# First ffn of a four-layer network: quantized numbers read as 16-bit halves of their words, and the gate products issued ahead of the up products

## The reference

```python
def act_qdq(x):
    qmax = 2.0 ** (ACT_BITS - 1) - 1.0
    scale = jnp.maximum(jnp.max(jnp.abs(x)) / qmax, 1e-12)
    return jnp.clip(jnp.round(x / scale), -qmax - 1.0, qmax) * scale
x = act_qdq(x)
up = act_qdq(x @ lpbq_dequant(w_up).T)
gate = act_qdq(x @ lpbq_dequant(w_gate).T)
sig = fixed_qdq_u16(jax.nn.sigmoid(gate))
gate = act_qdq(gate * sig)
o = act_qdq(gate * up)
return o @ lpbq_dequant(w_down).T
```

## Time and profile before

| | us |
|---|---|
| median of three runs | 1404.43 |
| lowest, highest | 1403.75, 1405.94 |
| the profiled execution | 1409.03 |
| its span on the core | 1407.2 |
| PE busy | 1245.4 (88%) |
| DVE busy | 861.9 (61%) |
| ACT busy | 675.2 (48%) |
| POOL busy | 291.5 (21%) |

### The profile page before, as it was taken

One profiled execution on the slowest core, in us unless ns is written; L12 is line 12 of the kernel. 1 busy time (PEld: TensorE's weight loads), 2 busy tenths in 40 slices (PEclk: granted clock), 3 DMA queues, 4 the chain that ended last, 5 costly groups with the idle time before them and its releaser, 6 DMA issues.

```text
span 1407.2 us, 26467 instructions
## 1 busy us (share of the span) xinstructions
PE 1245.4 (88%) x9327; PEld 964.6 (69%) x9327; DVE 861.9 (61%) x1828; ACT 675.2 (48%) x1358; POOL 291.5 (21%) x502
## 2 busy tenths in 40 slices
PE   3889980688999889999888999899999998898999
PEld 2555630256888889887777888498888754555877
DVE  3879768754456566656676565566554566764242
ACT  1556858545443334444444444234444375665553
POOL 1799400120002233230000013044320111100000
PEclk9999995899999999999999999999999999999999
DMA  8000010131050313104006001032120000000000
GB/s 312 1 2 2 2 75 0 65 137 61 1 202 23 113 46 100 48 25 177 30 1 264 40 7 48 21 111 68 33 94 2 1 2 2 1 2 1 0 15 16
DMA packets 42606, 75.71 MB, mean 54 GB/s; under 512 B 3816, under 2 KB 33520, under 8 KB 41584
## 3 DMA queue, kind: packets, MB, share of 16 engines
q1 hardware_dynamic: 38384, 65.62, 12.7%
q0 software_dynamic: 4096, 8.40, 1.9%
HBM read 59.72 MB, written 14.29 MB: 53 GB/s over the span
## 4 chain that ended last, share of the span: by engine, by line
PE 69%; DVE 15%; ACT 7%; issue 4%; POOL 2%; DVEq 1%; DMA 1%; SPq 0%; ACTq 0%; POOLq 0%
PE bank L1674 7%; PE bank L1663 7%; PE bank L1659 6%; PE bank L1718 5%; PE bank L1650 3%; PE bank L1445 3%; PE bank L1511 3%; PE bank L1728 3%; PE bank L1450 3%; PE bank L1451 2%; PE bank L1452 2%; PE bank L1643 2%; PE bank L1645 2%; PE bank L1644 2%; PE bank L1527 2%
## 5 line engine op out<-in xcount | busy, mean ns | idle before, releaser
L1911 ACT ACTIVATE SC<-bank 128x512 f32<-128x512 f32 x192 | 114.3, 595 | 218.1 <-PE bank L1659 123.3
L1998 DVE SCALAR_TENSOR_TENSOR SC<-bank,SM,SC 128x512 f32<-128x512 f32 x128 | 95.8, 749 | 125.0 <-PE bank L1663 108.6
L1674 PE MATMUL bank<-A,SC 128*128 x1024 | 137.0, 277 | 7.2 <-DVE SC L1998 6.2
L1663 PE MATMUL bank<-X,SC 128*128 128x128 f32 x1024 | 136.6, 276 | 6.1 <-DVE SC L2277 5.6
L1659 PE MATMUL bank<-X,SC 128*128 128x128 f32 x1024 | 135.6, 275 | 2.9 <-ACT SC L1895 2.8
L1659 PEld LDWEIGHTS bank<-X,SC 128*128 128x128 f32 x1024 | 126.3, 192 | 16.2 <-issue 10.2
L1674 PEld LDWEIGHTS bank<-A,SC 128*128 128x128 f32 x1024 | 125.4, 192 | 16.6 <-issue 15.7
L1663 PEld LDWEIGHTS bank<-X,SC 128*128 128x128 f32 x1024 | 124.5, 192 | 8.5 <-DVE SC L2277 8.4
L1718 PE MATMUL bank<-A 128*128 128x128 f32 x736 | 99.7, 279 | 11.0 <-DVE A L2427 5.5
L1811 ACT ACTIVATE A<-bank,SM 128x128 f32<-128x128 f32 x256 | 73.6, 382 | 66.6 <-DVE SM L2094 66.4
L1718 PEld LDWEIGHTS bank<-A 128*128 128x128 f32 x736 | 89.8, 192 | 15.3 <-ACT A L1936 8.4
(11 more groups left out here) (324 smaller groups left out, 2630.3 us busy)
## 6 DMA issues: line engine op xcount, KB each, us to landing
A<-in_moe SPq DMA_DIRECT2D x36, 768.0 KB, 10.2
A<-xs SPq DMA_DIRECT2D x20, 256.0 KB, 3.5
ys<-A SPq DMA_DIRECT2D x20, 256.0 KB, 2.4
BW<-in_l1f SPq DMA_DIRECT2D x2, 2048.0 KB, 7.8
BW<-in_l2f SPq DMA_DIRECT2D x1, 3456.0 KB, 12.0
BW<-in_l1c SPq DMA_DIRECT2D x1, 3072.0 KB, 16.3
BW<-in_l3f SPq DMA_DIRECT2D x1, 2816.0 KB, 9.6
A<-in_l1c SPq DMA_DIRECT2D x1, 2560.0 KB, 8.9
```

The costliest lines, as they stand in the source:

```text
L1663: m = e.matmul(at["pu"].ap[:, cut(q)], wx[:, cut(4 + q)], x, start=True, stop=True)
L1674: m = e.matmul(o, at["h"].ap[:, cut(q)], W[:, bass.ds(r + (1024 + 128 * q), 128)], start=k == 0 and q == 0, stop=k == 1 and q == 3)
L1911: e.activation(at["h"].ap, at["pg"].ap, ACT.Gelu_apprx_tanh).then_inc(at["gelu"][0], 1)
L1998: return e.scalar_tensor_tensor(out=o, in0=a, scalar=s, in1=b, op0=o1, op1=o2)
```

## The change

It changes six things, all in the first ffn.

1. After `g0`, `upq` and `p0` a tile holds `MAGIC` plus a whole number below 32768 in magnitude. The new helper `codes` reads the lower 16 bits of each fp32 word as an int16, which is that whole number, with a step of two elements. So nothing subtracts `MAGIC` any more: `g1`, the DVE half of `upq` and the second ACT instruction of `p0` are gone. The int16 number is read by `g2`, `g4` and `p1`.
2. The factors that those instructions multiplied by move: `g2` takes the gate's scale as its scale operand, the others move into the scales (`unit` in `scale2`, small extra multiplications of one column).
3. `p1` is one `tensor_tensor` on DVE for all twelve tiles; the three POOL multiplications are gone, and an empty stage before `p3` too.
4. The twelve gate products come first, then the gate's `scale1`, two up products, and `scale2`.
5. The other ten up products, with their ACT copies and DVE maxima, are hung onto stages of the gate items, two in each of five rounds; then the up half's `scale1`, `scale2`, and one `upq` per round.
6. Of the twelve `upq`, five run in the gate stage, two between the halves of the gate product's `scale_of`, and five beside the first five `p0`.

```diff
+def codes(ap):
+    m, t = ap.shape[1], ap.shape[2]
+    return ap.bitcast(mybir.dt.int16).rearrange("p b (t h) -> p b t h", h=2)[:, :, :, 0]
...
+        def scale_begin(mx, n, ready, unit=()):
             r1, r2, scl, inv = sm(1), sm(1), sm(1), sm(1)
             at = step("scale1", mx=mx[:, 0:n], r1=r1, r2=r2, ready=ready)
...
+            def rest():
+                bt = step("scale2", r2=r2, scl=scl, inv=inv, all=at["all"], unit=[(x, tick("f0_vec")) for x in unit])
...
-        for n in range(NC):
-            for m in range(6):
...
-        gs, gi, tg = scale_of(mg, 12, td_)
-        us, ui, tu_ = scale_of(mu, 12, td_)
...
+        for n, m in nms:
+            t_gate = up_product(n, m)
+        up_products = [(n, m + 3) for n, m in nms]
+        gs, gi, tg = scale_of(mg, 12, t_gate, (), lambda: [up_product(*up_products.pop(0)) for _ in range(2)])
...
-            return ([], [f0, f1, f2, f3, f4, f5], None)
+            return ([], [f0, f2, f3, f4, f5], None)
...
-        g2s, g2i, t2 = scale_of(mg2, 12, sig["g2"], lambda: [up_step(*nm) for nm in nms[:8]])
-        for nm in nms[8:]:
-            up_step(*nm)
+        def beside_gate(k):
+            for _ in range(2):
+                if up_products:
+                    sig["u"] = up_product(*up_products.pop(0))
+            if k == 5:
+                up_scale["rest"] = scale_begin(mu, 12, sig["u"])
+            if k == 6:
+                up_scale["s"], up_scale["inv"], up_scale["t"] = up_scale["rest"]()
+            if k >= 7:
+                up_step(*nms[k - 7])
...
+        for k in range(12):
+            x, at = (k, 1) if k < 3 else (k - 3, 4)
+            gates[x] = with_products(gates[x], at, k)
+        in_order(gates, done)
+        g2s, g2i, t2 = scale_of(mg2, 12, sig["g2"], [gs], lambda: [up_step(*nm) for nm in nms[5:7]])
...
-            return ([], [f0, f1, lambda: None, f3], None)
-
-        in_order([prod_item(n, m) for n, m in nms], done)
-        osc, oiv, t3 = scale_of(mo, 12, sig["o"])
+            return ([], [f0, f1, f3], None)
+
+        in_order([with_up(prod_item(*nm), 0, nms[k + 7]) if k < 5 else prod_item(*nm) for k, nm in enumerate(nms)], done)
+        osc, oiv, t3 = scale_of(mo, 12, sig["o"], [g2s, up_scale["s"]])
...
-                    e.activation(v4(at["s"].ap), at["G"], ACT.Sigmoid).then_inc(at["t"][0], 1)
+                    w.wait_ge(*at["ready"])
+                    e.activation(v4(at["s"].ap), codes(at["G"]), ACT.Sigmoid, scale=at["gs"]).then_inc(at["t"][0], 1)
...
-                    e.activation(at["G"], at["G"], ACT.Identity, scale=at["g2i"], bias=MAG).then_inc(at["q"][0], 1)
-                    w.wait_ge(*at["q"])
-                    e.activation(at["G"], at["G"], ACT.Identity, bias=NMAG).then_inc(at["t"][0], 1)
+                    e.activation(at["G"], at["G"], ACT.Identity, scale=at["g2i"], bias=MAG).then_inc(at["t"][0], 1)
...
+                    for x, t in at["unit"]:
+                        e.tensor_tensor(at["r2"], at["r2"], x, ALU.mult).then_inc(t[0], 1)
+                        w.wait_ge(*t)
...
+                    for (x, _), t in zip(at["unit"], at["back"]):
+                        w.wait_ge(*prev)
+                        e.tensor_tensor(at["inv"], at["inv"], x, ALU.mult).then_inc(t[0], 1)
+                        prev = t
...
-                    ts(at["G"], at["G"], MAGIC, at["gs"], ALU.subtract, ALU.mult).then_inc(at["t"][0], 1)
...
-                    stt(at["G"], v4(at["s"].ap), 192.0, at["G"], ALU.subtract, ALU.mult).then_inc(at["t"][0], 1)
+                    stt(at["G"], v4(at["s"].ap), 192.0, codes(at["G"]), ALU.subtract, ALU.mult).then_inc(at["t"][0], 1)
...
-                    ts(at["Uq"], at["Uq"], MAGIC, at["us"], ALU.subtract, ALU.mult).then_inc(at["t"][0], 1)
...
-                    if at["pooled"]:
-                        e.tensor_scalar(at["G"], at["G"], at["g2s"], None, ALU.mult).then_inc(at["t"][0], 1)
-                    else:
-                        stt(at["G"], at["G"], at["g2s"], at["Uq"], ALU.mult, ALU.mult).then_inc(at["t"][0], 1)
+                    e.tensor_tensor(at["G"], codes(at["G"]), codes(at["Uq"]), ALU.mult).then_inc(at["t"][0], 1)
```

More of the change, by code:

```diff
@@ L545, in build @@
         GG = A0[:, 6144:12288].rearrange("p (m b t) -> p m b t", m=3, b=16)
-        MAG, NMAG = sm(1), sm(1)
+        MAG = sm(1)
         SQ = Ring([A1[:, 512 * k:512 * k + 512] for k in range(4)])
         nms = [(n, m) for n in range(NC) for m in range(3)]
-        def scale_of(mx, n, ready, between=None):
+        def scale_begin(mx, n, ready, unit=()):
             r1, r2, scl, inv = sm(1), sm(1), sm(1), sm(1)
@@ L553, in scale_of @@
             at["red"], at["all"] = tick("f0_vec"), tick("f0_all")
+            def rest():
+                bt = step("scale2", r2=r2, scl=scl, inv=inv, all=at["all"], unit=[(x, tick("f0_vec")) for x in unit])
+                bt["scl_t"], bt["inv_t"] = tick("f0_vec"), tick("f0_vec")
+                bt["back"] = [tick("f0_vec") for _ in unit]
+                bt["t"] = (bt["back"] or [bt["inv_t"]])[-1]
+                return scl, inv, bt["t"]
+            return rest
+        def scale_of(mx, n, ready, unit=(), between=None):
+            rest = scale_begin(mx, n, ready, unit)
             if between is not None:
                 between()
-            bt = step("scale2", r2=r2, scl=scl, inv=inv, all=at["all"])
-            bt["scl_t"], bt["t"] = tick("f0_vec"), tick("f0_vec")
-            return scl, inv, bt["t"]
+            return rest()
         mx, mu, mg, mg2, mo = sm(4), sm(12), sm(12), sm(12), sm(12)
@@ L572, in build, with up_product @@
             tq.append(at["t"])
-        for n in range(NC):
-            for m in range(6):
[L575 to L581, removed]
-        gs, gi, tg = scale_of(mg, 12, td_)
-        us, ui, tu_ = scale_of(mu, 12, td_)
+        def up_product(n, m):
+            at = step("f0_up", n=n, m=m, y=tq[n], fw=sig["fw"], pa=RA.take(), dst=(UU if m >= 3 else GG)[:, m % 3, 4 * n:4 * n + 4, :],
+                      mx=(mu if m >= 3 else mg)[:, 3 * n + m % 3:3 * n + m % 3 + 1])
+            at["mm"] = sig["Yfree", n] = tick("f0_mm")
+            at["ev"] = tick("f0_act")
+            RA.give(at["pa"], at["ev"])
+            at["t"] = tick("f0_vec")
+            return at["t"]
+        for n, m in nms:
+            t_gate = up_product(n, m)
+        up_products = [(n, m + 3) for n, m in nms]
+        gs, gi, tg = scale_of(mg, 12, t_gate, (), lambda: [up_product(*up_products.pop(0)) for _ in range(2)])
+        up_scale = {}
         def gu(n, m):
@@ L594, in f0 @@
                 at["t"] = u["t"] = tick("f0_act")
-            def f1():
-                at = step("g1", G=G, gs=gs, prev=u["t"], ready=tg)
-                at["t"] = u["t"] = tick("f0_vec")
             def f2():
-                at = step("g2", G=G, prev=u["t"], s=SQ.take())
+                at = step("g2", G=G, gs=gs, prev=u["t"], ready=tg, s=SQ.take())
                 u["s"] = at["s"]
@@ L622, in up_step, with with_up, with_products @@
             _, Uq = gu(n, m)
[L623 to L627, removed]
-        g2s, g2i, t2 = scale_of(mg2, 12, sig["g2"], lambda: [up_step(*nm) for nm in nms[:8]])
-        for nm in nms[8:]:
-            up_step(*nm)
+            at = step("upq", Uq=Uq, ui=up_scale["inv"], ready=up_scale["t"])
+            at["t"] = tu[n, m] = tick("f0_act")
+        def with_up(item, at, nm):
+            needs, stages, gives = item
+            return (needs, stages[:at] + [lambda f=stages[at]: (f(), up_step(*nm))] + stages[at + 1:], gives)
+        def beside_gate(k):
[8 more added lines that the diff above has]
+                up_step(*nms[k - 7])
+        def with_products(item, at, k):
+            needs, stages, gives = item
+            return (needs, stages[:at] + [lambda f=stages[at]: (f(), beside_gate(k))] + stages[at + 1:], gives)
+        gates = [gate_item(*nm) for nm in nms]
+        for k in range(12):
[3 more added lines that the diff above has]
+        g2s, g2i, t2 = scale_of(mg2, 12, sig["g2"], [gs], lambda: [up_step(*nm) for nm in nms[5:7]])
         def prod_item(n, m):
@@ L637, in f0 @@
                 at = step("p0", G=G, g2i=g2i, ready=t2)
-                at["q"], at["t"] = tick("f0_act"), tick("f0_act")
-                u["t"] = at["t"]
+                at["t"] = u["t"] = tick("f0_act")
             def f1():
-                pooled = m == 1 and n < 3
-                at = step("p1", G=G, Uq=Uq, g2s=g2s, pooled=pooled, prev=u["t"], tu=tu[n, m])
+                at = step("p1", G=G, Uq=Uq, prev=u["t"], tu=tu[n, m])
                 at["t"] = u["t"] = tick("f0_vec")
-                if pooled:
-                    at["tp"] = u["t"] = tick("f0_ppool")
             def f3():
@@ L1843, in _ @@
                     w.wait_ge(*at["prev"])
-                    e.activation(v4(at["s"].ap), at["G"], ACT.Sigmoid).then_inc(at["t"][0], 1)
+                    w.wait_ge(*at["ready"])
```

(7 more changed lines are left out.)

12 lines of the change are left out of this document (3 added, 9 removed).

## The result

The changed kernel takes 1395.73 us (median of four runs, 1394.95 to 1398.26); the kernel before, timed beside it once more, 1405.16. The ratio is 0.9933 with a 95% interval of 0.9920 to 0.9945: 9.4 us, or 0.7%, faster. The prediction said 1394.6. A later comparison with five rounds on one chip gave 0.9930 (0.9917 to 0.9943).

A forecast was written before the change was run, and what follows sets the result against it. DVE and ACT were taken to bound the ffn's middle while TensorE idles. The terms -9.3 + 4.2 - 2.2 - 3.2 + 0.8 give -9.7, kept as 9.8 us: median 1404.4 to 1394.6 us, range 1391.0 to 1401.5.

The forecast's parts named there:

- Products, 9.3 less: Start of the ffn: with the gate products first, g0 begins at about 201.0 us, saving 9.3 us.
- Gate stage, 4.2 more: Gate's quantization: DVE loses g1, gets ten up maxima and idles 4.0 us at the start; 30.9 us against 26.7.
- The sigmoid with a scale operand, 0.70: Gate stage on ACT: g2 with its scale read from memory takes 0.70 us, bounds 0.62 to 0.80.
- Turn, 2.2 less: Between gate and product stages: without eight upq on DVE, 3.7 us becomes 1.4.
- Product stage, 3.2 less: Product stage: five tiles at ACT's 1.42 us, then DVE's 1.20 a tile; 17.0 us against 20.2.
- Last scale, 0.8 more: Last scale before dq: four small multiplications at 0.19 us each on the path add 0.8 us.
- 16-bit reads at the word's rate: Reads of int16 at every second place cost the same as contiguous two-source rows, 681 and 692 ns.
- Rivals one and two: Stepped reads pay the far-step price (1401.2 to 1402.2 us, chance 0.10), or run at half rate (1413.1 us, chance 0.04).
- rival one: Gate and product stages: stepped reads cost 0.32 us more a tile; the gain shrinks to 2.2 to 3.2 us, chance 0.10.
- Rival three: TensorE's clock low for all 24 down instructions: costs up to 10.8 us and leaves 1405.4 us, chance 0.03.
- Rival four: Gate stage: up copies, sigmoids and g0 in ACT's queue hold each other; gain 5 us, 1399.6 us, chance 0.07.
- a gap of 2.2 us is safe: Before the down products: the clock dropped some 4.5 us after TensorE's work, so a 2.2 us gap keeps it at 1.00.

The follow-up runs named there:

- e6_mid0: The changed kernel without the two up products between scale1 and scale2 of the gate; first down product 66.8 us after the first product, 0.4 later.
- e3_steps: The changed kernel with two maxima read in steps of two and of 128 words; first down product 69.7 us after the first product, 3.3 later.
- e5_cold: The changed kernel without the four warming products after the eighth p3; first down product still at 66.4 us, last down step 1.6 us later.
- e8_best: The changed kernel with the sigmoid table load and the last scale's unit-scale product made early; 1394.49 us, ratio 0.9911 to the kernel before.

## Why the prediction was right

Point by point, in its own steps, from the profiled execution:

- **Products, 9.3 less.** From the first product 13.9 us to `g0` for 23.2, 9.3. The two maxima ahead of `scale2` are there, and `e6_mid0` shows their price (0.9) and what they save. `g0` itself began at 200.57 and not at 201.0, because everything began 0.48 earlier: the first product at 186.67 for 187.15, ahead of any changed step and within what this start varies by.
- **Gate stage, 4.2 more.** 30.9 us for 26.7; the split is right too: idle 4.1, 1.0 and 0.7 at DVE's first three rounds (4.0, 1.1, 0.8 forecast), then DVE full.
- **The sigmoid with a scale operand, 0.70.** 726 ns, inside the bounds 0.62 to 0.80.
- **Turn, 2.2 less.** 1.5 for 3.7 us.
- **Product stage, 3.2 less.** 16.9 for 20.2 us, 3.3.
- **Last scale, 0.8 more.** From `scale1` at 249.86 to `dq` at 251.67 it is 1.8 us, before 1.1 (260.93 to 262.03), 0.7 more.
- **16-bit reads at the word's rate.** 686 ns for `p1`. Rivals one and two have fallen; rival one's price was right and its condition wrong.
- **Rival three.** The down products ran at full clock, 1.00 from the first of them on. The mean of 0.98 in the last window comes from the warming products, which ran at the half clock until about 250.4. The gap behind the warming products did not grow to 2.2, as the prediction had it, but stayed 1.3, since they ran longer at the half clock, 6.03 us for 5.29:

```profile
245.71 6.03 PE L1602 MATMUL bank<-CC 128*128 128x512 f32 x8 [33.83 <-DVE SM L2035]
...
253.06 3.27 PE L1608 MATMUL bank<-A,BW 128*128 128x512 f32 x7 [1.32 <-DVE A L2029]
```

- **Rival four.** ACT's queue paced the first rounds as summed, to 0.1 us, and no more.

The sum for the ffn was 9.8 and the trace has 9.9 (66.4 for 76.3). The rest of the 10.8 in the span is the 0.5 ahead of the first product and 0.5 behind the first down product; the medians have 9.4. That the median came within 1.1 us of the forecast is in part luck, since the part behind the ffn took between 1139.6 and 1149.0 us in the eleven executions; the agreement of the stages is not, as the ffn's time came out alike each time that a kernel was profiled twice (66.4 and 66.4, 64.6 and 64.6). Two things in the reasoning were wrong without harm to the number. The clock's price in rival three was too high, above. And the inference that a gap of 2.2 us is safe does not hold: see below. What the prediction did not say, though its own terms held it, is that the order of the products, which the title names, is worth 2.3 us of the 9.9, and that together with the new places of `upq` it is worth nothing without the halves.

## What to carry to other kernels

Add up each engine's queue for each stage, with distances between starts and not durations; the larger sum, plus the idle start until its first input, gave the length of the gate stage of the changed kernel to 0.1 us before it ran (30.9), and 23.7 us, on record for the halves alone, came out too. For the order alone only a total was on record, and it was 1.4 us too low. Moving work out from under one engine's stage into the next one gains only if the engine that bounds the next stage has room: the new order of the products was worth 2.3 us with the halves, and with the new places of `upq` nothing without them. And a gain of 1.8 us in one stage of a program of 1400 us has to be read at the stage, because the part behind varied by more than that from one execution to another.

## What the runs showed of the hardware

TensorE's clock can fall after a short idle gap, and need not. In the changed kernel TensorE had nothing to do from 202.35 to 204.65 us, 2.3 us. The clock was still full when it went on, and was at half (1.2 GHz) from 206 to about 209.5 while it worked:

```profile
202.00:204.00 2.00, 0.35 (x1) 0.00 (x0) 0.00 (x0) 1.97 (x3) 0.00 (x0) 1.00 0.00 0
204.00:206.00 2.00, 1.35 (x3) 0.68 (x4) 1.28 (x2) 2.00 (x5) 0.00 (x0) 1.00 0.00 0
206.00:208.00 2.00, 2.00 (x4) 0.55 (x3) 1.08 (x2) 2.00 (x5) 0.00 (x0) 0.51 0.00 0
208.00:210.00 2.00, 2.00 (x5) 0.82 (x4) 1.33 (x4) 2.00 (x5) 0.00 (x0) 0.63 0.00 0
```

The same gap of 2.3 us was followed by such a fall in the second profile of the changed kernel, in `e3_steps` and in `e5_cold`. But in `e6_mid0` a longer one at this place, 3.1 us, with shorter pauses of 0.3 us behind it, was followed by full clock:

```profile
200.30:203.40 3.10, 0.04 (x1) 0.00 (x0) 0.00 (x1) 3.07 (x5) 0.00 (x0) 1.00 0.00 0
203.40:212.30 8.90, 7.93 (x16) 2.71 (x16) 7.22 (x14) 8.90 (x16) 0.00 (x0) 1.00 0.00 0
```

In `e8_best` a gap of 1.9 us ahead of the down products was followed by full clock, and in `e3_steps` one of 2.0 us by a mean of 0.70 in the first 5.6 us of them. So the length of the gap alone doesn't settle it here; what does, these traces don't show.

GpSimd's reduction over the partitions, 0.35 to 0.38 us elsewhere in the changed kernel's ffn, lasted 1.05 for the up half's scale, while DVE worked without a pause; DVE came to the instruction that uses its result only after it had ended. In the kernel before, the one beside eight `upq` on DVE lasted 0.73.
